# A fused two-layer block on one core: low halves and unpacking in the first feed-forward, merged turns and later value blocks in the second attention, roots and the end in the second feed-forward

## What is computed

```python
def _L0_ffn_ref(x, Wr, br, W1, W2):          # 16 blocks of 128 hidden units, the best 4 kept per token
    mask = ...                               # 1.0 for the top 4 of softmax(x @ Wr.T + br)
    h = jax.nn.gelu(einsum(x, W1b)) * mask
    return einsum(h, W2b)

def _L1_attn_ref(hidden_states, ...):        # 32 heads of 64, 8 key-value heads, rotary, causal
    scores = jnp.einsum('bhqd,bhkd->bhqk', q, kf) / 8
    attn = jax.nn.softmax(jnp.where(causal, scores, min), axis=-1)
    out = jnp.einsum('bhqk,bhkd->bhqd', attn, v)
    return out @ o_w.T

def _L1_ffn_ref(x, gate_up_packed, gate_up_scales, down_packed, down_scales):
    w_gu, w_down = ...                       # 4-bit codes looked up, times a scale per group of 128
    h = jax.nn.silu(gate) * up               # 1408 hidden units
    y = einsum(h, w_down)
    return y / jnp.sqrt(jnp.mean(y * y, axis=-1, keepdims=True) + 1e-6)
```

## Time and profile before

| | us |
|---|---|
| median of 3 runs | 2230.88 (2230.74 to 2238.21) |
| the profiled execution | 2236.44 |
| its span, first to last instruction | 2234.7 |
| TensorE busy | 2069.3 (93%) |
| VectorE busy | 1536.4 (69%) |
| ScalarE busy | 844.8 (38%) |
| GpSimd busy | 441.3 (20%) |

### The profile page before, as it was taken

How to read it: one execution, slowest core, us unless ns; L and a number is a source line. 1 busy time by engine, 2 the same in 40 slices (tenths; PEclk the granted TensorE clock), 3 DMA queues, 4 the chain that set the end, 5 groups by cost and what they waited for, 6 DMA issues and landing times. The chain is left out here.

```text
span 2234.7 us, 52900 instructions
## 1 busy us (share of the span) xinstructions
PE 2069.3 (93%) x21680; PEld 1461.3 (65%) x21680; DVE 1536.4 (69%) x2407; ACT 844.8 (38%) x1773; POOL 441.3 (20%) x280
## 2 busy tenths in 40 slices
PE   7999979999997999979899998999988899999997
PEld 5777758887786788724444544445445688787776
DVE  6544333798976355589999999999995330577776
ACT  4322122222223200055655665555653322244443
POOL 0111112223220154400110010100101444211111
PEclk9999989999998999969999999999999899999999
DMA  5122244344327633424444454444543655320101
GB/s 185 58 96 77 76 150 170 104 135 135 126 77 283 184 113 128 141 81 121 127 121 125 119 143 128 120 123 116 142 124 102 226 172 177 104 76 27 49 1 38
DMA packets 209147, 268.18 MB, mean 120 GB/s; under 512 B 42336, under 2 KB 123552, under 8 KB 206240
## 3 DMA queue, kind: packets, MB, share of 16 engines
q1 hardware_dynamic: 208064, 264.85, 38.3%
q10 hardware_dynamic: 864, 0.21, 0.0%
HBM read 181.81 MB, written 83.17 MB: 119 GB/s over the span
## 5 line engine op out<-in xcount | busy, mean ns | idle before, releaser
L1688 ACT ACTIVATE a_prob<-ps,a_nmax 128x256 f32<-128x256 f32 (+7 forms) x512 | 377.1, 739 | 311.9 <-DVE a_nmax L1727 214.5
L1797 PE MATMUL ps<-xacc 64*128 64x512 f32 (+5 forms) x1536 | 382.5, 540 | 69.5 <-ACT a_prob L1688 63.2
L1727 DVE TENSOR_REDUCE a_nmax<-ps 128x1 f32<-128x1024 f32 (+3 forms) x256 | 256.3, 1001 | 31.3 <-PE ps L1797 30.9
L1797 PEld LDWEIGHTS ps<-xacc 64*128 64x128 f32 x1536 | 144.1, 194 | 187.2 <-ACT a_prob L1688 127.8
L1748 DVE STREAM_TRANSPOSE a_pt_long<-a_prob 128x768 f32<-128x768 f32 (+1 forms) x256 | 237.8, 929 | 0.0
L2111 DVE SCALAR_TENSOR_TENSOR f_part<-ps,f_gu_scale,f_part 128x512 f32<-128x512 f32 x264 | 184.9, 746 | 66.7 <-PE ps L2158 53.4
L1812 PE MATMUL ps<-a_pt_long,xacc 32*64 32x256 f32 (+1 forms) x6144 | 206.7, 377 | 6.0 <-issue 3.9
L1716 POOL TENSOR_TENSOR a_o<-a_o,a_rd 128x1024 f32<-128x1024 f32 x31 | 73.0, 2356 | 696.3 <-ACT a_o L1698 686.3
L1812 PEld LDWEIGHTS ps<-a_pt_long,xacc 32*64 32x64 f32 x6144 | 121.0, 133 | 107.8 <-issue 98.3
L945 POOL TENSOR_TENSOR f_hT_lo<-f_h,f_hT_hi 128x512 fp32r<-128x512 f32 x64 | 94.2, 1480 | 276.6 <-ACT f_hT_hi L928 276.6
L1794 PE MATMUL ps<-xacc 64*128 64x128 bf16 x1024 | 112.5, 225 | 6.1 <-ACT a_prob L1688 6.0
(11 more groups left out here) (234 smaller groups left out, 4463.1 us busy)
## 6 DMA issues: line engine op xcount, KB each, us to landing
xacc<-scratch_QT SPq DMA_DIRECT2D x512, 64.0 KB, 2.1
scratch_QT<-k_qo SPq DMA_DIRECT2D x64, 256.0 KB, 2.3
xacc<-scratch_V SPq DMA_DIRECT2D x64, 256.0 KB, 4.8
a_rd<-scratch_R SPq DMA_DIRECT2D x64, 256.0 KB, 4.4
scratch_OT<-a_o SPq DMA_DIRECT2D x32, 512.0 KB, 3.9
o_of<-scratch_OT SPq DMA_DIRECT2D x30, 512.0 KB, 4.0
f_block<-in_packed SPq DMA_DIRECT2D x33, 256.0 KB, 3.4
xacc<-in_x SPq DMA_DIRECT2D x8, 1024.0 KB, 6.4
```

Of the source, the lines that this page charges most:

```text
L1688: last = nc.scalar.activation(prob[:, n % PRING, s].rearrange("p (a w) -> p a w", w=w), SC[n % 2][:, a, 0:w], ACT.Exp, bias=nmax[:, n % 4, ...
L1727: nc.vector.tensor_reduce(nmax[:, n % 4, 0:1], SC[n % 2][:, :, 0:width(0, t)], AX.XY, ALU.max, negate=True).then_inc(maxed, 1)
L1797: last = pe.matmul(sc[:, a, 0:w], q[r, slot, heads[a * hf], :], kt[r, b, keys], start=not masked, stop=True, skip_group_check=True)
```

## The change

In the first feed-forward VectorE makes the low halves of blocks 0 to 2, each behind the next block's mask product, and GpSimd only that of block 3 (its own semaphore `h_last`); four unpacking operations (6 to 9) stand ahead of the split of the weights instead of behind it; the shift table counts on the semaphore of the scales. In the second attention one instruction turns both heads of a short step, and the value blocks are dealt to other steps. In the second feed-forward the squares stand in step 2 behind the high half, the root in step 3 ahead of the gate, the additions two in step 4 and two in step 5, and the last chunk is squared, rooted and added tile by tile straight from PSUM, with the table of the root loaded ahead.

GpSimd and VectorE in the first feed-forward:

```diff
-                        for b in range(BPQ):
-                            pool.wait_ge(h_hi.sem, h_hi.now(it, b + 1))
...
+                        b = BPQ - 1
+                        pool.wait_ge(h_hi.sem, h_hi.now(c + q * NCH, b + 1))
...
+                            if b:
+                                dve.wait_ge(h_hi.sem, h_hi.now(it, b))
+                                nc.vector.tensor_tensor(hT[1][:, b - 1, :], h[:, (b - 1) % 2, :],
+                                                        hT[0][:, b - 1, :].bitcast(F32), ALU.subtract
+                                                        ).then_inc(h_lo.sem, 1)
                             if b < BPQ - 1:
                                 unpack_some(range(2 * b, 2 * b + 2))
+                        unpack_some(range(2 * BPQ - 2, 2 * BPQ + 2))
                         if q + 1 < NQ:
                             split((q + 1) % 2, c, c + (KC + q * NCH))
...
-                        unpack_some(range(2 * BPQ - 2, OPS))
+                        unpack_some(range(2 * BPQ + 2, OPS))
```

The second attention's tables and VectorE's turn:

```diff
-SHORT_VALUES = {26: (0, 15, 14, 13, 12), 27: (11, 10, 9, 8), 28: (7, 6), 29: (5, 4), 30: (3, 2), 31: (1,)}
+SHORT_VALUES = {26: (0, 15, 14, 13), 27: (12, 11, 10, 9), 28: (8, 7), 29: (6, 5), 30: (4, 3), 31: (2,), 32: (1,)}
-LONG_VALUES = {34: range(0, 2), 35: range(2, 4), 36: range(4, 6), 37: range(6, 8), 38: range(8, 10), 39: range(10, 11),
-               40: range(11, 13), 41: range(13, 15), 42: range(15, 18), 43: range(18, 21), 44: range(21, 24),
-               45: range(24, 28), 46: range(28, 32)}
-SHORT_LEFT = {32: (0, 1)}
+LONG_VALUES = {35: range(0, 2), 36: range(2, 4), 37: range(4, 6), 38: range(6, 8), 39: range(8, 10), 40: range(10, 12),
+               41: range(12, 14), 42: range(14, 16), 43: range(16, 19), 44: range(19, 22), 45: range(22, 26),
+               46: range(26, 30), 47: range(30, 32)}
+SHORT_LEFT = {33: (0, 1)}
-SHORT_STORE, LONG_STORE = 35, 51
-SHORT_INVERSE, LONG_INVERSE = 29, 36
+SHORT_STORE, LONG_STORE = 36, 51
+SHORT_INVERSE, LONG_INVERSE = 29, 37
...
-                        if hf:
-                            last = nc.vector.transpose(pt_short[:, 0:blocks, h, t, :], src)
...
+                    if hf:
+                        src = prob[:, n % PRING, 0:2 * blocks * 32].rearrange("p (h j k) -> p h j k", h=2, k=32)
+                        last = nc.vector.transpose(
+                            pt_short[:, 0:blocks, heads[0]:heads[0] + 2, t, :].rearrange("p j h q -> p h j q"), src)
```

ScalarE in the second feed-forward (`squares(c)` holds the four squares that stood in `root(c)`), then VectorE (`finish_last` inverts and adds each tile of the last chunk as soon as its root is there):

```diff
+                def last_roots():
+                    act.wait_ge(ready, LAST)
+                    nc.scalar.activation(square[:, 0:1], eps[:], ACT.Sqrt).then_inc(rooted, 1)
+                    for t in range(TPC):
+                        act.wait_ge(y_done, TPC * (NF - 1) + t + 1)
+                        act.wait_ge(rooted, LAST + 2 * t + 1)
+                        nc.scalar.activation(square[:], YB[t], ACT.Square, accum_out=ss[:, t:t + 1]
+                                             ).then_inc(rooted, 1)
+                        act.wait_ge(rooted, LAST + 2 * t + 2)
+                        nc.scalar.activation(rms[:, t:t + 1], ss[:, t:t + 1], ACT.Sqrt, bias=eps[:], scale=1.0 / C
+                                             ).then_inc(rooted, 1)
...
-                        gate(s)
+                        if c and n == 2:
+                            squares(c - 1)
                         if c and n == 3:
                             root(c - 1)
-                for t in range(TPC):
-                    copy_y(NCH - 1, t)
-                root(NCH - 1)
+                        gate(s)
+                last_roots()
...
                     if c and n == 4:
-                        finish(c - 1)
-                finish(NCH - 1)
+                        invert(c - 1)
+                        finish(c - 1, (0, 1))
+                    if c and n == 5:
+                        finish(c - 1, (2, 3))
+                finish_last()
```

59 lines of the change are left out of this document (37 added, 22 removed).

## The result

| | before | after |
|---|---|---|
| median (6 runs each) | 2232.38 us (2230.74 to 2238.21) | 2221.36 us (2216.93 to 2224.59) |
| ratio, 95% interval | | 0.9947 (0.9931 to 0.9963) |
| the profiled execution, its span | 2236.44, 2234.7 us | 2224.16, 2222.4 us |

The account below looks back on a forecast made before the run. TensorE was taken to bound the kernel, with VectorE setting the attention's pace up to step 10. Terms -4.2, +10.8, -13.8 and -4.7 sum to -11.9 us: 2230.9 - 11.9 = 2219 us, range 2204 to 2227.

Parts of the forecast that it names:

- What bounds the kernel: All three changed stages: an edit is worth only what it removes of TensorE's gaps or adds to its row of work.
- First feed-forward, -4.2: First feed-forward: VectorE's pass gets 2.7 us shorter, so TensorE's four stalls go; -4.2 us, bounds 0 and -4.2.
- Merged turns, 0: Second attention: 9 to 19 us of VectorE's time saved, but where TensorE or a score is waited for; counted 0.
- rival (d): Second attention: the merged turn, writing with one more stride, runs slower than two; up to 2261 us, chance 0.07.
- Value blocks, +10.8: Second attention: blocks moved into TensorE's full stretch add 0.72 us a unit over 15 units; +10.8 us, bounds 0 and 16.
- Rival (a): Second attention: the value-block delay is swallowed and the merged turns count; 2199 to 2208, say 2204 us, chance 0.17.
- rival (c): Second attention: steps 9 to 11 fall to half clock in every unit instead of five; +17, 2236 us, chance 0.09.
- Chunk turns, -13.8: Second feed-forward, turns between 512-token chunks: TensorE's six waits, restarts and half-clock pieces go; -13.8 us, bounds -14 and -8.
- Rival (b): Second feed-forward, chunk turns: ScalarE's table loads cost more than their own time; +4.6, 2224 us, chance 0.09.
- End, -4.7: End of the second feed-forward: the chain after the last matmul falls from 10.3 to 5.6 us; -4.7, bounds -3.5 and -5.5.
- The sum: Whole kernel: all terms together -11.9 us, profiled execution 2236.4 to 2224.5 us, median 2219 us; chance of the forecast 0.58.

Follow-up runs that it names:

- the old tables with the merged turns: The changed kernel with the second attention's value blocks back in the steps of the kernel before; 2214.1 us, ratio 0.9905 to the kernel before.
- the four runs: Runs of the changed kernel with short value blocks 4 to 1 dealt one each over steps 6 to 9; 2211.7 us, ratio 0.9897 to the kernel before.

## Why the prediction was right

- **What bounds the kernel.** The statement that the attention has two owners, VectorE up to step 10 and TensorE from step 11 on, carried the forecast, and the runs bear it out in both directions: two blocks more in TensorE's part (1.05 us of work) +0.66 us, six blocks fewer (2.8 us of work) -2.2 us, VectorE's own time less by 0.4 us: nothing.
- **First feed-forward, -4.2.** Measured -4.7. The stalls went as forecast. The working had VectorE late by about 1 us a pass (1.2 by its rows) and the two savings at 2.7 us; they gave 2.2. The price of 1.1 us for each GpSimd operation was that of the longest product; over all 64 mask products the mean fell by 0.18 us. The term didn't hang on it, and the working didn't say that either saving would have done alone.
- **Merged turns, 0.** Right: no unit length changed by more than 0.06 us. The time of a turn (1.05 ns an element) was right within 2%; rival (d) had nothing in it.
- **Value blocks, +10.8.** Measured +12.7. The term by unit was right (15 x 0.66 = 9.9 instead of 10.8). What was missed is the number of pieces at half clock: I kept five, the profile of after has seven, 2 x 1.4 = 2.8 us. The reason that I gave, "still three scores without value blocks in a row", counts steps, and the runs say more: other profiles with the same tables had 5 to 8, the old tables with the merged turns had 8, and one block in step 9 made it 0. The number differs between profiles of the same tables, so the five of one profile was no constant to carry over, and that the changed tables themselves brought the two more is not shown. Rival (a), the delay swallowed, fell with the first row of the unit; rival (c), a piece in every unit, didn't come (7 of 16 have one), but its mechanism was the live one of the four.
- **Chunk turns, -13.8.** Measured -14.4. The squares fitted into step 2 with 0.57 us to spare. Undone one by one, the parts were 11.3 (ScalarE) and 4.1 us (VectorE), 15.4 in sum; the forecast's share for VectorE's waits (2.0 us and what goes with them) was too small. That a wait behind another one was partly paid for by it in the kernel before would explain this; no run tests it. The working also had the root and both loads fit into one stretch. The second load came late: it starts at 2021.64, and VectorE's product waits 1.37 us for the SiLU behind it. It was luck that VectorE had that much to spare: TensorE waited for nothing.
- **Rival (b), loads that cost more than themselves.** It fell: the root of 2019.04 starts 0.02 us after the end of its load of 1.28 us. By the Trainium skill (ScalarE: Activation LUTs, What ACT_TABLE_LOAD costs) a switch would cost some 2.66 us with its drain; neither this row nor that of 2213.53, at once behind the last load (2212.24, 1.28 us), shows a drain.
- **End, -4.7.** Measured -5.1, in the profiles and by undoing it. The working took 0.94 us for the last addition from the chunk turn; at the end one takes 0.75 (and before 2.74 / 4 = 0.69), so the chain is 5.3 instead of 5.6 us. It also called TensorE idle in the 10.3 us before; its last product starts at 2223.51, behind the first copy. The first is the 0.3 us by which the term was off; the second doesn't touch it.
- **The sum** was met within 0.4 us on the profiled execution, and that closeness is partly luck: the attention cost 1.9 us more than forecast, and the four other stages together came out 2.3 us better, one of them (-0.8) without a reason given. Inside the attention, too, 0.9 us less by unit stand against 2.8 us more by pieces. The median came out 2.4 us above the forecast because the profiled execution of after lies 2.8 us over its own median where that of before lay 4 to 5.6 over it. Part of that scatter may be the pieces at half clock, 1.4 us each: without them the four runs lie within 1.0 us.

## What to carry to other kernels

Where two engines take turns in setting the pace within a period, cut the period at the place where the owner changes, and write the busy time of both beside the length of each part: work that moves from one part to the other is worth most of its time there (here 0.66 us of 1.05 one way, 2.2 of 2.8 the other), and work saved on the engine that still waits somewhere behind it in the period was worth nothing here. A hole in TensorE's row that costs nothing by itself can still be worth filling, if the clock falls behind it and the full row comes next. And after a forecast of "+0.7 a unit, because blocks were moved there", the natural next question is what the opposite move gives; it gave more than three times what the whole change did.

## What the runs showed of the hardware

- TensorE's clock fell from 2.4 to 1.2 GHz in seven of fourteen units behind a stretch in which it had been busy for 1.66 of 3.40 us, and in none where one block more made it 2.27 of 3.40. Such a piece cost 1.4 us of the unit. What decided between the seven and the others isn't shown.
- In rows of short products (32 rows by 64 to 256 columns, 16 ns apart at the shortest) TensorE stood still for 0.2 to 2.0 us with nothing to wait for: 6.8 us in ten pauses in the kernel with six long blocks early, which has 80 such products in one step, 1.5 us in four with the changed tables. With the short blocks spread and at most 64 in a step they still came to 4.9 us in eight, so the length of the row alone doesn't explain them. They come at different units in different runs. The cause isn't settled.
- A table load ran ahead of its instruction's wait in two kernels and not in the changed one. There the load for the SiLU behind a root starts only at 2021.64, when the gate's own wait is over, though ScalarE had been idle for 2.30 us; VectorE's product waited 1.37 us for it, three times (4.1 us in sum), which is hidden here. Before, the load stood at 2021.34, at once behind the high half, and was over 1.1 us before the SiLU started:

```profile
2021.34 1.28 ACT L2050 ACT_TABLE_LOAD   x1
2023.75 0.63 ACT L2050 ACTIVATE f_sl<-f_part 128x512 f32<-128x512 f32 x1 [1.12 <-DVE f_part L2111]
```

  In the kernel with the squares behind the gate it runs ahead as well (2028.31, SiLU at 2031.77). The changed `root` ends with a wait for the root itself, just ahead of the gate's two; that this third wait holds the load back fits the three traces, but no run tests it.
- A GpSimd subtraction beside it made VectorE's product of two operands dearer, 875 ns in the mean with 64 of them (before, and again with the low halves back on GpSimd) and 691 with 16; one took 1.78 where another took 0.68 us.
